# Gathers of a graph network issued in quarters that wait for the turn, and with a pause in the middle of each group

## The chip, the cores and the metric

The kernel runs on one core of a Trainium2 chip. The metric is the device time in microseconds of one execution. The core has five engines with queues of their own: TensorE (PE; its weight loads are PEld), VectorE (DVE), ScalarE (ACT), GpSimd (POOL) and SyncE (SP), which here only issues transfers. They meet through semaphores: an instruction, or a transfer that has landed, adds to one, and another engine waits until it has reached a value.

## The reference

Four graph layers over 6250 nodes with 256 features and 106250 edges in order of their destination. Cut to what matters:

```python
edge_index = jnp.stack([src, dst])
h = jnp.maximum(_layernorm(x), 0.0)
# two convolution layers, for each: x = x + relu(segment_sum(h[row] * norm[:, None], col) + b),
# with h = layer_norm(x) @ W.T; after the second one x @ Wp.T + bp
x = x + _L0_gnn_ref(h, edge_index, edge_weight, ...)
h = jnp.maximum(_layernorm(x), 0.0)
# attention layer with 4 heads, then a transformer layer with one head:
#   alpha = segment_softmax(leaky_relu(a_src[src] + a_dst[dst]), dst)
#   x1    = prelu(segment_sum(h[src] * alpha, dst) + bias)
#   alpha2 = segment_softmax(q[dst] . k[src] * scale, dst)
#   out   = prelu(segment_sum(v[src] * alpha2, dst) + x1 @ Wskip + bskip)
x = x + _L1_gnn_ref(h, edge_index, ...)
```

## The kernel before

The edges are cut into 52 groups of 2048 (`NGW` = 52): 128 partitions times 16 columns (`UW` = 16). The kernel runs four layers one after the other, each as a loop of 52 turns, one turn for each group. In this data a group's destinations lie within one window of 128 nodes (the work on a window's nodes is recorded 53 times in a layer: 52 groups and the end); loops for more windows stand in the code.

For each group GpSimd issues 16 gathers, one for each column: each fetches 128 rows of a node table in HBM (256 to 264 numbers of 4 bytes), by the source indices of the column, into `G[:, b, u]`. `G` has four buffers (`NBW` = 4), so the gathers of group g go where group g - 4 was, and they are issued while the turn of group g - 3 runs. A quarter is four columns (`QW` = 4). GpSimd does nothing but issue these gathers.

- **Convolution layers 1 and 2** (`first_layer`, `second_layer`). GpSimd waits, ahead of a group's first gather, until ACT has added to `s_done` for group g - 4 (L800, L1114), then issues all 16 (L227, L849). In a turn VectorE makes 16 one-hot matrices `oh` (L577, L947), TensorE multiplies each with a column of `G` and sums into `ps` (L727, L1069; it signals each quarter through `s_ohu`), ScalarE copies the sum to `stage` (the eviction, L799, L1112; it waits for all four signals), and TensorE, ScalarE and VectorE work out the window's nodes from it. The landing of each quarter has its own semaphore, `s_g[b][q]`.
- **Attention layer** (`gat_layer`, called layer 3 here). VectorE adds the logits `L` once the whole group has landed (`s_g[b]`, one semaphore for a group) and the scores `psA` are there, runs maxima along the edges (`F`, `W`), and signals `s_s1`; TensorE turns the ends (L1586, L1587, signal `s_rt`), VectorE carries the maxima over the partitions (`run`, `Out`, signal `s_s2`), TensorE turns them back (L1594, L1595, signal `s_bt`), VectorE works out `M` and `z`, ACT the exponentials. Then VectorE writes `Gp` from `M` (L1490, signal `s_lastM`) and weighs `G` into `Gp` in four quarters (L1390, signal `s_gp` each). One turn later TensorE adds up `oh` times `Gp` (L1561), a quarter at a time, each with the signal `s_aq`. VectorE makes the next group's `oh` quarter q only when `s_aq` tells that the old one was read (L1279). TensorE then makes the next group's scores (L1519) and the node's products (L1527 to L1539). GpSimd waits once in a group, for `s_gp` of group g - 4, and issues all 16 gathers (L1192).
- **Transformer layer** (`transformer_layer`, layer 4). Not touched. Its gathers already wait at each quarter, for `s_aq` of that quarter, and at the first also for `s_ok`.

SyncE loads and stores the nodes' rows of each window. An engine's queue is in program order; nothing but the semaphores orders the engines against each other.

Of the kernel before, what the change touches and what calls it, by code (L numbers as in the profile page):

```python
# [43 lines left out]
NBW = 4  # L44
QW = 4
# [72 lines left out]
def first_layer(nc, m, a):  # L118
# [13 lines left out]
    with ExitStack() as c:  # L132
# [48 lines left out]
        s_g = [[sem(f"gath{b}{q}") for q in range(UW // QW)] for b in range(NBW)]  # L181
# [17 lines left out]
        @block.gpsimd  # L199
        def _(pool):  # L200
            nc.gpsimd.memset(m.ones[:], 1.0)
            nc.gpsimd.memset(m.eps[:], LN_EPS)
            nc.gpsimd.memset(m.ident[:], 0.0).then_inc(s_set, 1)
            pool.wait_ge(s_set, 1)
            nc.gpsimd.affine_select(out=m.ident[:], in_=m.ident[:], compare_op=ALU.not_equal, fill=1.0,
                                    base=0, pattern=[[-1, P]], channel_multiplier=1)
            nc.gpsimd.iota(m.iota[:], [[1, P]], base=0, channel_multiplier=0, allow_small_or_imprecise_dtypes=True)
            nc.gpsimd.iota(m.iotap[:], [[1, 1]], base=0, channel_multiplier=1, allow_small_or_imprecise_dtypes=True)
            nc.gpsimd.memset(stage[:], 0.0)
            nc.gpsimd.memset(al[:], 0.0)  # L210
            nc.gpsimd.memset(h[:, :, D:AW], 0.0)
            nc.gpsimd.memset(zrow[:], 0.0).then_inc(s_set, 1)
            nc.gpsimd.memset(acc, 0.0).then_inc(s_accz, 1)
            pool.wait_ge(s_si, 16)
            pool.wait_ge(s_z1, 16)
            pool.wait_ge(s_ast, 16)
            for j in range(NLB):
                pool.wait_ge(s_t1[j], 16)
            for g in range(NGW):
                b = g % NBW  # L220
                width = D if g < NBW else AW
                if g >= NBW:
                    pool.wait_ge(s_done, g - NBW + 1)
                if g == NBW:
                    pool.wait_ge(s_col, 16)
                for u in range(UW):
                    pool.indirect_dma_start(G[:, b, u, 0:width], None, m.t1,  # L227
                                            IOA(ap=m.srcI[:, g * UW + u:g * UW + u + 1], axis=0)).then_inc(s_g[b][u // QW], 16)

# [575 lines left out]
def second_layer(nc, m, a_in):  # L805
# [5 lines left out]
    with ExitStack() as c:  # L811
# [14 lines left out]
        s_g = [[sem(f"gath{b}{q}") for q in range(UW // QW)] for b in range(NBW)]  # L826
# [14 lines left out]
        @block.gpsimd  # L841
        def _(pool):
            nc.gpsimd.memset(stage[:], 0.0).then_inc(s_zero, 1)
            for g in range(NGW):
                b = g % NBW
                if g >= NBW:
                    pool.wait_ge(s_done, g - NBW + 1)
                for u in range(UW):
                    pool.indirect_dma_start(G[:, b, u, :], None, table, IOA(ap=m.srcI[:, g * UW + u:g * UW + u + 1],  # L849
                                                                            axis=0)).then_inc(s_g[b][u // QW], 16)  # L850

# [268 lines left out]
def gat_layer(nc, m):  # L1120

    tag = "g3_"
    LD, ST, NQ = 16, 48, UW // QW
    GL = UW * 16
    SW = HC + 1
    with ExitStack() as c:
# [21 lines left out]
        s_g = [sem(f"gath{b}") for b in range(NBW)]  # L1148
# [32 lines left out]
        @block.gpsimd  # L1181
        def _(pool):
            nc.gpsimd.memset(run[:], -BIG)
            nc.gpsimd.memset(Lb[:], -BIG)
            nc.gpsimd.memset(t4[:], 1.0)
            nc.gpsimd.memset(stage[:], 0.0).then_inc(s_zero, 1)
            for g in range(NGW):
                b = g % NBW
                if g >= NBW:
                    pool.wait_ge(s_gp, (g - NBW + 1) * NQ)  # L1190
                for u in range(UW):
                    pool.indirect_dma_start(G[:, b, u, :], None, m.t3, IOA(ap=m.srcI[:, g * UW + u:g * UW + u + 1],  # L1192
                                                                           axis=0)).then_inc(s_g[b], 16)

# [1179 lines left out]
```

## Time and profile before

| | |
|---|---|
| time, median of 3 runs | 6131.06 us (6126.41 to 6134.06) |
| profiled execution: its time | 6161.81 us |
| its span, first to last instruction | 6160.0 us |
| mean granted TensorE clock | 0.761 of full speed |
| PE busy | 3909.5 us (63%) |
| PEld busy | 2847.9 us (46%) |
| DVE busy | 2717.3 us (44%) |
| ACT busy | 718.7 us (12%) |
| POOL busy | 3225.9 us (52%) |

No engine is busy all the time. "Busy" leaves out waits, branches and the issuing of SyncE's transfers. A wait in the profile is named after the last update of a semaphore that the profile can find; semaphore numbers are used again by the next layer, so a wait can be put down to a tile of another layer. "issue" and "remote" are waits for which it finds no instruction. The ends of matmuls are modelled.

### The profile page before, as it was taken

What the parts mean: (1) busy time and instruction counts of PE and PEld (TensorE: products, weight loads), DVE (VectorE), ACT (ScalarE), POOL (GpSimd) and SP (SyncE); (2) the same over time, 40 slices, a digit from 0 to 9 for tenths busy, and PEclk for the clock granted to TensorE, in tenths of its full rate; (3) what the DMA queues carried; (4) which work ended last, traced back from release to release, by engine and by line L of the source; (5) the groups of instructions that cost most, each with busy time, mean ns of one, the idle gap of its engine ahead of it and who ended that gap; (6) DMA issues with size and microseconds to landing.
All of it is one profiled execution on the core that took longest, in us unless ns stands there. A gap on an engine that the chain in (4) does not pass through costs nothing. (4 is left out here: it accounts for less than half of the span.)

```text
span 6160.0 us, 73788 instructions
## 1 busy us (share of the span) xinstructions
PE 3909.5 (63%) x14574; PEld 2847.9 (46%) x14575; DVE 2717.3 (44%) x9904; ACT 718.7 (12%) x2361; POOL 3225.9 (52%) x3351
## 2 busy tenths in 40 slices
PE   3555555563665566654676766666674777777777
PEld 2343434342444344443555555555552555555555
DVE  5443434343233323332444444444453555555555
ACT  3000000000000000000111111101010222121222
POOL 5466666645555555655444444444423555555553
PEclk8677777776777777776777777777776888888889
DMA  7344444433333333333333333333322344444442
GB/s 182 80 107 106 107 106 107 106 87 90 108 108 107 105 106 107 108 99 90 89 91 100 91 98 91 98 94 96 96 75 85 109 122 115 119 119 114 121 114 84
DMA packets 334355, 636.43 MB, mean 103 GB/s; under 512 B 86166, under 2 KB 213124, under 8 KB 333828
## 3 DMA queue, kind: packets, MB, share of 16 engines
q0 software_dynamic: 159744, 441.43, 27.7%
q1 hardware_dynamic: 170437, 185.56, 9.7%
q8 instruction: 177, 2.90, 0.2%
q10 hardware_dynamic: 3648, 3.67, 0.2%
q14 instruction: 349, 2.86, 0.2%
HBM read 565.59 MB, written 64.79 MB: 102 GB/s over the span
## 5 line engine op out<-in xcount | busy, mean ns | idle before, releaser
L1192 POOL DMA_INDIRECT g_G<-t,srcI x832 | 810.2, 974 | 925.1 <-DVE g_Gp L1390 686.1
L1785 POOL DMA_INDIRECT g_G<-t,srcI x832 | 791.5, 951 | 626.3 <-PE g_ps L2152 365.5
L227 POOL DMA_INDIRECT g_G<-t,srcI x832 | 818.5, 984 | 518.8 <-issue 238.5
L849 POOL DMA_INDIRECT g_G<-t,srcI x832 | 796.4, 957 | 541.2 <-ACTq L1114 302.3
L2142 PE MATMUL g_psA<-g_win,g_ohT 128*128 128x257 f32 x1664 | 613.9, 456 | 369.6 <-issue 187.0
L727 PE MATMUL g_ps<-g_G,g_oh 128*128 128x257 f32 x1664 | 550.3, 496 | 141.7 <-DVE g_oh L577 139.3
L1519 PE MATMUL g_psA<-g_win,g_ohT 128*128 128x4 f32 x1664 | 345.1, 328 | 439.0 <-issue 429.1
L1887 DVE CUSTOM_DVE_ANT_0 g_junk<-g_G,g_psA 128x257 f32<-128x257 f32 x832 | 348.0, 418 | 569.2 <-DMA g_G<-t,srcI 245.8
L1519 PEld LDWEIGHTS g_psA<-g_win,g_ohT 128*128 128x128 f32 x1664 | 360.1, 317 | 459.5 <-issue 459.2
L2152 PE MATMUL g_ps<-g_G,g_oh 128*128 128x257 f32 x1664 | 560.1, 423 | 2.3 <-issue 2.3
L2142 PEld LDWEIGHTS g_psA<-g_win,g_ohT 128*128 128x128 f32 x1664 | 319.1, 216 | 503.0 <-issue 232.1
L727 PEld LDWEIGHTS g_ps<-g_G,g_oh 128*128 128x128 f32 x1664 | 412.3, 256 | 287.5 <-DVE g_oh L577 182.6
L1069 PE MATMUL g_ps<-g_G,g_oh 128*128 128x256 f32 x1664 | 517.7, 460 | 0.0
L1069 PEld LDWEIGHTS g_ps<-g_G,g_oh 128*128 128x128 f32 x1664 | 379.2, 237 | 97.2 <-issue 34.8
L1561 PE MATMUL g_ps<-g_Gp,g_oh 128*128 128x264 f32 x1664 | 408.1, 393 | 15.9 <-issue 15.8
L2152 PEld LDWEIGHTS g_ps<-g_G,g_oh 128*128 128x128 f32 x1664 | 353.5, 215 | 86.7 <-issue 26.2
L1279 DVE TENSOR_TENSOR g_oh<-iota,g_relx 128x512 f32<-128x512 f32 x208 | 135.5, 689 | 562.5 <-DMA g_G<-t,srcI 519.7
L1561 PEld LDWEIGHTS g_ps<-g_Gp,g_oh 128*128 128x128 f32 x1664 | 310.8, 192 | 95.8 <-issue 43.8
L947 DVE TENSOR_SCALAR g_oh<-iota,g_relx,g_wx 128x128 f32<-128x128 f32 x832 | 229.0, 350 | 141.5 <-issue 75.5
L584 DVE SCALAR_TENSOR_TENSOR g_a<-g_own,g_stage 128x256 f32<-128x256 f32 x53 | 25.7, 485 | 566.6 <-ACT g_stage L799 565.1
L964 DVE TENSOR_TENSOR g_o<-g_psP,g_xb 128x256 f32<-128x256 f32 x53 | 22.5, 425 | 535.7 <-DMA g_srow<-srow 444.7
L577 DVE TENSOR_SCALAR g_oh<-iota,g_relx,g_wx 128x128 f32<-128x128 f32 x832 | 239.9, 363 | 32.5 <-issue 22.6
(373 smaller groups left out, 5050.1 us busy)
## 6 DMA issues: line engine op xcount, KB each, us to landing
g_G<-t,srcI POOLq DMA_INDIRECT x3328
g_relb<-relrow SPq DMA_DIRECT2D x104, 512.0 KB
t<-g_t SPq DMA_DIRECT2D x53, 132.0 KB
g_rec<-t SPq DMA_DIRECT2D x53, 132.0 KB
g_own<-t SPq DMA_DIRECT2D x53, 129.5 KB
x<-g_o SPq DMA_DIRECT2D x53, 128.5 KB
g_rec<-x SPq DMA_DIRECT2D x53, 128.5 KB
t<-g_t4r SPq DMA_DIRECT2D x53, 128.5 KB
```

The lines of the kernel that those rows point to most:

```text
L227: pool.indirect_dma_start(G[:, b, u, 0:width], None, m.t1, IOA(ap=m.srcI[:, g * UW + u:g * UW + u + 1], axis=0)).then_inc(s_g[b][u // QW], 16)
L577: nc.vector.tensor_scalar(oh[:, u, :], m.iota[:], relx[:, u:u + 1], wx[:, u:u + 1], ALU.is_equal, ALU.mult).then_inc(s_oh, 1)
L727: last = nc.tensor.matmul(ps[:, 0:CW], oh[:, u, :], G[:, b, u, 0:CW], start=(u == 0), stop=(u == UW - 1))
L849: pool.indirect_dma_start(G[:, b, u, :], None, table, IOA(ap=m.srcI[:, g * UW + u:g * UW + u + 1], axis=0)).then_inc(s_g[b][u // QW], 16)
L1069: last = nc.tensor.matmul(ps[:, 0:D], oh[:, u, :], G[:, b, u, :], start=(u == 0), stop=(u == UW - 1))
L1192: pool.indirect_dma_start(G[:, b, u, :], None, m.t3, IOA(ap=m.srcI[:, g * UW + u:g * UW + u + 1], axis=0)).then_inc(s_g[b], 16)
L1519: last = nc.tensor.matmul(psA[:, u * H:u * H + H], ohT[:, u, :], win[:, b % 2, :], start=True, stop=True)
L1561: last = nc.tensor.matmul(ps[:, 0:AGW], oh[:, b1, u, :], Gp[:, b1, u, :], start=(u == 0), stop=(u == UW - 1))
L1785: pool.indirect_dma_start(G[:, b, u, :], None, m.t4, IOA(ap=m.srcI[:, g * UW + u:g * UW + u + 1], axis=0)).then_inc(s_g[b][u // QW], 16)
L1887: nc.vector.tensor_tensor_reduce(out=junk[:, u % 2, :], in0=G[:, b, u, :], in1=psA[:, u % 2, 0:RW], scale=1.0, scalar=0.0, op0=ALU.mult, o ...
L2142: nc.tensor.matmul(psA[:, u % 2, 0:RW], ohT[:, u, :], win[:, r, :], start=True, stop=True).then_inc(s_pa, 1)
L2152: last = nc.tensor.matmul(ps[:, r, 0:RW], oh[:, b2, u, :], G[:, b2, u, :], start=(u == 0), stop=(u == UW - 1))
```

## The change

- In both convolution layers GpSimd waits once more in each group from the fifth on: ahead of the ninth gather, until the second quarter of this same group (gathers 5 to 8) has landed.
- In the attention layer the single wait ahead of a group is split into four, one ahead of each quarter: the first as before (`s_gp`: group g - 4 has been weighed), the second for `s_aq` of the second quarter of group g - 4 (TensorE has added up half of it), the third for `s_s2` and the fourth for `s_lastM` of group g - 3, whose turn is running.

```diff
--- before.py
+++ after.py
@@ -224,6 +224,8 @@
                 if g == NBW:
                     pool.wait_ge(s_col, 16)
                 for u in range(UW):
+                    if g >= NBW and u == 2 * QW:
+                        pool.wait_ge(s_g[b][1], (g // NBW + 1) * 16 * QW)
                     pool.indirect_dma_start(G[:, b, u, 0:width], None, m.t1,
                                             IOA(ap=m.srcI[:, g * UW + u:g * UW + u + 1], axis=0)).then_inc(s_g[b][u // QW], 16)
 
@@ -846,6 +848,8 @@
                 if g >= NBW:
                     pool.wait_ge(s_done, g - NBW + 1)
                 for u in range(UW):
+                    if g >= NBW and u == 2 * QW:
+                        pool.wait_ge(s_g[b][1], (g // NBW + 1) * 16 * QW)
                     pool.indirect_dma_start(G[:, b, u, :], None, table, IOA(ap=m.srcI[:, g * UW + u:g * UW + u + 1],
                                                                             axis=0)).then_inc(s_g[b][u // QW], 16)
 
@@ -1186,9 +1190,16 @@
             nc.gpsimd.memset(stage[:], 0.0).then_inc(s_zero, 1)
             for g in range(NGW):
                 b = g % NBW
-                if g >= NBW:
-                    pool.wait_ge(s_gp, (g - NBW + 1) * NQ)
                 for u in range(UW):
+                    if g >= NBW:
+                        if u == 0:
+                            pool.wait_ge(s_gp, (g - NBW + 1) * NQ)
+                        elif u == QW:
+                            pool.wait_ge(s_aq, (g - NBW) * NQ + 2)
+                        elif u == 2 * QW:
+                            pool.wait_ge(s_s2, g - NBW + 2)
+                        elif u == 3 * QW:
+                            pool.wait_ge(s_lastM, g - NBW + 2)
                     pool.indirect_dma_start(G[:, b, u, :], None, m.t3, IOA(ap=m.srcI[:, g * UW + u:g * UW + u + 1],
                                                                            axis=0)).then_inc(s_g[b], 16)
```

## Rows read from the trace of the kernel before

**Rows 1.** One line's instructions: attention gathers, duration in ns, first and last start.

```profile
L1192 POOL DMA_INDIRECT g_G<-t,srcI x832: 940/946/3132, 2825.7 to 4559.9; - x167
```

**Rows 2.** Waits, whole run: us in total, times, longest us.

```profile
ACT g_stage L799 <- remote: 807.7, 48, 17.6
...
DVE g_oh L1279 <- DMA g_G<-t,srcI: 519.7, 55, 14.2
...
DVE g_o L964 <- DMA g_srow<-srow: 444.7, 38, 50.4
```

**Rows 3.** ScalarE's timeline, evictions: start us, us, what [idle before].

```profile
211.49 0.39 ACT L799 ACTIVATE g_stage<-g_ps 128x257 f32<-128x257 f32 x1 [11.34 <-PE g_ps L727]
...
1349.11 0.39 ACT L799 ACTIVATE g_stage<-g_ps 128x257 f32<-128x257 f32 x1 [16.86 <-remote]
...
1402.38 0.39 ACT L799 ACTIVATE g_stage<-g_ps 128x257 f32<-128x257 f32 x1 [11.34 <-PE g_ps L727]
...
1512.74 0.38 ACT L1112 ACTIVATE g_stage<-g_ps 128x256 f32<-128x256 f32 x1 [3.30 <-PE g_ps L1069]
...
2759.97 0.38 ACT L1112 ACTIVATE g_stage<-g_ps 128x256 f32<-128x256 f32 x1 [3.25 <-PE g_ps L1069]
...
2806.10 0.38 ACT L1112 ACTIVATE g_stage<-g_ps 128x256 f32<-128x256 f32 x1 [2.07 <-PE g_ps L1069]
...
2947.47 0.39 ACT L1654 ACTIVATE g_stage<-g_ps 128x264 f32<-128x264 f32 x1 [0.16 <-DVE g_v L1339]
...
4568.17 0.39 ACT L1654 ACTIVATE g_stage<-g_ps 128x264 f32<-128x264 f32 x1 [0.20 <-DVE g_v L1339]
...
4632.10 0.39 ACT L1654 ACTIVATE g_stage<-g_ps 128x264 f32<-128x264 f32 x1 [0.20 <-issue]
...
5320.39 0.39 ACT L2240 ACTIVATE g_stage<-g_ps 128x257 f32<-128x257 f32 x1 [2.19 <-PE g_ps L2152]
...
5428.56 0.39 ACT L2240 ACTIVATE g_stage<-g_ps 128x257 f32<-128x257 f32 x1 [6.48 <-PE g_ps L2152]
...
6087.60 0.39 ACT L2240 ACTIVATE g_stage<-g_ps 128x257 f32<-128x257 f32 x1 [1.57 <-PE g_ps L2152]
...
6130.22 0.39 ACT L2240 ACTIVATE g_stage<-g_ps 128x257 f32<-128x257 f32 x1 [0.33 <-PE g_ps L2152]
```

**Rows 4.** Timeline of one turn of layer 1: GpSimd, ScalarE, TensorE.

```profile
852.00 0.94 POOL L227 DMA_INDIRECT g_G<-t,srcI  x1 [3.83 <-ACTq L800]
...
870.93 0.95 POOL L227 DMA_INDIRECT g_G<-t,srcI  x1 [0.30 <-issue]
...
868.93 0.70 PE L727 MATMUL g_ps<-g_G,g_oh 128*128 128x257 f32 x2
...
875.10 0.39 ACT L799 ACTIVATE g_stage<-g_ps 128x257 f32<-128x257 f32 x1 [16.71 <-remote]
```

**Rows 5.** Timeline of one turn of the attention layer: GpSimd, TensorE, VectorE.

```profile
3573.68 0.94 POOL L1192 DMA_INDIRECT g_G<-t,srcI  x1 [15.01 <-DVE g_Gp L1390]
...
3584.45 0.71 PE L1561 MATMUL g_ps<-g_Gp,g_oh 128*128 128x264 f32 x2
...
3587.39 0.17 PE L1519 MATMUL g_psA<-g_win,g_ohT 128*128 128x4 f32 x1 [1.99 <-issue]
...
3596.70 1.89 DVE L1279 TENSOR_TENSOR g_oh<-iota,g_relx 128x512 f32<-128x512 f32 x3 [12.81 <-DMA g_G<-t,srcI]
```

**Rows 6.** Timeline in layer 4: first and last of eight gathers, VectorE.

```profile
5299.91 0.95 POOL L1785 DMA_INDIRECT g_G<-t,srcI  x1 [2.12 <-PE g_ps L2152]
...
5308.72 0.95 POOL L1785 DMA_INDIRECT g_G<-t,srcI  x1 [0.30 <-issue]
...
5311.47 0.42 DVE L1887 CUSTOM_DVE_ANT_0 g_junk<-g_G,g_psA 128x257 f32<-128x257 f32 x1 [2.91 <-DMA g_G<-t,srcI]
```

**Rows 7.** Timeline, attention layer's first group: its sixteenth gather and who awaits it.

```profile
2846.65 0.94 POOL L1192 DMA_INDIRECT g_G<-t,srcI  x1 [0.30 <-issue]
...
2849.57 0.27 DVE L1406 TENSOR_TENSOR g_L<-g_G,g_psA 128x64 f32<-128x64 f32 x1 [16.56 <-DMA g_G<-t,srcI]
```

## The prediction

> **What bounds the kernel now.** I read the page first, then the waits, then the timelines of single turns. The page shows no busy engine (PE 63%, POOL 52%), so the time lies in waits. The waits [rows 2] show where: ScalarE waits 807.7 us in 48 pieces, 16.8 us each, to evict layer 1's sum; VectorE waits 519.7 us in layer 3 to refill its one-hots; and 444.7 us in layer 2 for TensorE's second product. Two of these are named after a DMA, but the instructions wait for TensorE's signals (`s_aq`, `s_prod2`); I go by the code.
>
> The timelines say what those signals wait for. In layer 1 a group's first gather starts at 852.00, the last matmul of the running sum ends at 868.93 + 0.70 = 869.63, and nothing but TensorE's signal is missing; yet the eviction starts at 875.10, 5.5 us later and 23.10 us after the first gather [rows 4]. In layer 3 the matmuls of the sum end at 3585.16, but VectorE's refill of quarters 2 to 4 starts at 3596.70, 11.5 us later and 23.02 us after the first gather [rows 5]; TensorE's small score matmuls are meanwhile issued 2 us apart (1.99 us idle ahead of the one at 3587.39). In layer 4, whose gathers come in quarters already, eight in a row start at 5299.91, and the wait behind them ends at 5311.47, after 11.56 us [rows 6]. 23.10/16, 23.02/16 and 11.56/8 are all 1.44 us. So I read: while GpSimd gathers without a break, TensorE's signals are held back, and they are let go 1.44 us times the number of gathers after the first. GpSimd itself needs (870.93 - 852.00)/15 = 1.262 us a gather [rows 4], 20.19 us a group; the attention layer's gathers are the same in length, 946 ns of work each in the median of 832 [rows 1], and the rest is a 0.30 us gap ahead of each.
>
> How much this costs can be read off the end of each layer, where the last turns run with no gathers beside them. From eviction to eviction [rows 3]:
> - layer 1: (1349.11 - 211.49)/48 = 23.70 us with gathers, (1402.38 - 1349.11)/3 = 17.76 without
> - layer 2: (2759.97 - 1512.74)/48 = 25.98 and (2806.10 - 2759.97)/3 = 15.38
> - layer 3: (4568.17 - 2947.47)/47 = 34.48 and (4632.10 - 4568.17)/3 = 21.31
> - layer 4: (5428.56 - 5320.39)/4 = 27.04 and (6130.22 - 6087.60)/2 = 21.31
>
> Layers 1 to 3 bind themselves to it: the eviction (or the weighing, in layer 3) sets off the next burst of 16, and the burst holds back the next eviction.
>
> **Conv layers: the pause.** Nothing is removed; 48 waits are added in each layer. Behind the wait in GpSimd's queue stand only gathers, for data that is used three turns later. The wait's price is GpSimd's idle time. The one landing that an engine visibly waits for is that of layer 3's first group: its sixteenth gather starts at 2846.65, and VectorE goes on at 2849.57, 2.92 us later [rows 7]. The eighth gather of a group starts 7 x 1.262 = 8.83 us after the first, so it is known to have landed at 11.75 us; the ninth would have started at 10.09. The pause is 1.66 us, and a group takes GpSimd 20.19 + 1.66 = 21.85 us at least. That is the floor of a turn. The first eight's hold ends at 8 x 1.44 = 11.56 us, just within the pause, so the second half starts with the signals free. The Trainium skill (DMA: Bandwidth & Descriptors, "Anatomy of one DMA — SWDGE (gpsimd) path") fits such a transfer with 2.0 us plus bytes/436 GB/s, an estimate of 2.3 us for 128 KB; by it the pause would be 1.0 us and would end inside the first half's hold. The row has the longer time and decides.
>
> - Layer 1: between 23.70 (no gain) and 21.85. The sum's last matmul ends 17.63 us after the first gather [rows 4], 5.9 us into the second half. If that signal is held to the second half's end, 11.75 + 11.56 = 23.3 us, the turn is as long as before; if it gets through, evictions run ahead and the turn falls to the floor for good, as three buffers are in hand. I can't tell which, so I take the middle: 22.8, a gain of 0.9 x 48 = 43 us.
> - Layer 2: between 25.98 and 21.85. It loses twice in a turn, at the second product [rows 2] and at the eviction. The first is clearly in the first half and is freed by 11.56; the second is as in layer 1. Without holds its turn is only 15.38, so more margin is there than in layer 1. I take 23.2, two thirds of the way: 2.8 x 48 = 133 us.
>
> **Attention layer: four gates.** One wait in 48 groups becomes four. Again only gathers stand behind them. They need to be issued by the turn's end: 20.19 us of issuing fit into 34.48 and still into 22. The landing is needed two turns after the last gate, so lateness costs nothing. The gates fall like this in a turn: quarter 1 when the weighing ends, quarter 2 when half of the sum is added (some 8 to 10 us on, so quarter 1 stands alone and its hold is over at 4 x 1.44 = 5.8), quarter 3 at `s_s2`, which has then passed, so right behind quarter 2; quarter 4 at `s_lastM`, then the next quarter 1. So two groups of eight take the place of one of sixteen, each with a hold that ends at 11.56 instead of 23.02 us. The refill and `s_bt`, due some 5 us into the first eight, come up to 6.7 us late instead of 11.5.
>
> The nearest rows for the result are layer 4's: quarters, in fours and eights, and there a turn takes 27.04 - 21.31 = 5.7 us more than without gathers [rows 3]. With it layer 3's turn is 21.31 + 5.7 = 27.0, a gain of 7.4 x 47 = 350 us. Bounds: no gain at 34.48, and 22, where GpSimd's 20.19 and TensorE's 21.31 meet, 12.5 x 47 = 590 us.
>
> **Sum.** 43 + 133 + 350 = 526 us. The profiled execution would go from 6161.81 to 5636. It lies 30.75 us above the median 6131.06; with the same saving the median becomes 5605.
>
> **Rivals.**
> 1. *Layer 3's quarters join up* (5840). If `s_bt` comes through early, `s_lastM` comes before the hold of quarters 2 and 3 has ended, quarter 4 follows without a gap, then the next quarter 1: again 16 in a row and a hold of 23 us, now over the node's products. I reckon some 32 us a turn: 2.5 x 47 = 118, with the conv layers' 176, 294. For it: layer 3's plain turn is nearly as short as GpSimd's 20.19. Against it: held signals delay `s_lastM` themselves, which separates the bursts again.
> 2. *The pause doesn't take in the conv layers* (5780): the late signal stays held to 23.3 us in each turn, or the second half starts before the first's hold is over, as only 11.75 against 11.56 us speaks for it. Layer 3's 350 us remain.
> 3. *The waits have nothing to do with bursts* (6131, no change). Gatherless turns are shorter in all four layers, by 6 to 13 us, which speaks against it. The Trainium skill (SBUF — State Buffer, "Who interferes with whom") says that DMA never contends with a compute engine and that PE never waits on anyone; by that rule moving gathers about would change nothing. Rows 4 and 5 disagree with the rule as far as TensorE's signals go: 5.5 and 11.5 us between matmul and signal.
> 4. *Slower: the hold ends a fixed time after the last gather, wherever it is* (6290). In layer 1 the eviction starts 875.10 - 871.88 = 3.2 us after the last gather's end [rows 4]. If that is the law, the pause moves each eviction and so each turn by its 1.66 us: 96 x 1.66 = 159 us, layer 3 unchanged. It decides from any pause at all, since the next burst waits for the eviction. Against it: behind eight gathers it is 5311.47 - 5309.67 = 1.8 us [rows 6], not 3.2; the delay grows with the burst, as 1.44 - 1.262 = 0.18 us a gather does.
>
> **How the numbers follow.** Forecast 0.60, rival 1 0.16, rival 2 0.14, rival 3 0.04, rival 4 0.06. Under 0.2% (12 us) a measurement of this kernel can't tell a change from none. The forecast's own range is 5420 to 5720: layers 1 and 2 both at the floor give 89 + 198 instead of 176, and layer 3 anywhere from 25 to 29 a turn. The whole range is 5400 to 5850, which takes in rivals 1 and 2 and leaves 3 and 4 outside. Faster 0.90, same 0.04, slower 0.06.
>
> **What would show it.** In the profile after: GpSimd's ninth gather in the conv layers has an idle time of 1.5 to 2 us ahead of it. Layer 1's evictions come 21.9 to 23.7 us apart, layer 2's 21.9 to 24.5, layer 3's about 27, layer 4's 27.0 as before. The wait of L1279 falls from 519.7 us to below 250, that of L964 to below 300. In layer 3 GpSimd's gathers stand in fours and eights, not in sixteens. The prediction fails if layer 3's turn stays above 31, if signals are held as long behind eight gathers as behind sixteen, or if GpSimd becomes the bound of layer 3 with landings waited for at L1406.

## The result, and the profile after

The change makes the kernel slower: 6246.22 us (median of 4, 6226.23 to 6287.01) against 6130.16 (6126.41 to 6134.06), ratio 1.0205, 95% interval 1.0168 to 1.0242. The forecast was 5605 us. The profiled execution takes 6287.01 us, its span is 6285.1 us, and the mean granted clock is 0.734 (0.761 before).

ScalarE's timeline after, first and last eviction of layers 1 and 2, and in layer 3 the first one and the one 47 turns later (start us, us, what [idle before]):

```profile
212.04 0.39 ACT L801 ACTIVATE g_stage<-g_ps 128x257 f32<-128x257 f32 x1 [11.34 <-PE g_ps L729]
...
1397.52 0.39 ACT L801 ACTIVATE g_stage<-g_ps 128x257 f32<-128x257 f32 x1 [11.21 <-PE g_ps L729]
...
1508.76 0.38 ACT L1116 ACTIVATE g_stage<-g_ps 128x256 f32<-128x256 f32 x1 [4.27 <-PE g_ps L1073]
...
2838.84 0.38 ACT L1116 ACTIVATE g_stage<-g_ps 128x256 f32<-128x256 f32 x1 [2.06 <-PE g_ps L1073]
...
2964.70 0.39 ACT L1665 ACTIVATE g_stage<-g_ps 128x264 f32<-128x264 f32 x1 [0.16 <-issue]
...
4676.32 0.39 ACT L1665 ACTIVATE g_stage<-g_ps 128x264 f32<-128x264 f32 x1 [0.20 <-issue]
```

Against [rows 3]: layer 1 takes 1185.5 us instead of 1190.9, layer 2 1330.1 instead of 1293.4, and the 47 turns of layer 3 1711.6 instead of 1620.7 (36.42 us a turn instead of 34.48). So most of the loss is in the attention layer, some in layer 2. The profiled execution of before is some 30 us longer than its median, so small differences from it mean little: in the runs below that leave layer 1 alone it takes 1184.8 to 1185.9 us on the chips with the same time, as after the change. The waits after (us in total, times, longest):

```profile
POOL g_G L1203 <- PE g_ps L1572: 761.8, 48, 17.7
ACT g_lt L1653 <- remote: 653.4, 43, 15.7
...
PE g_psO L1546 <- ACT g_lt L1653: 471.7, 43, 11.4
...
DVE g_o L968 <- DMA g_srow<-srow: 339.1, 31, 48.8
...
DVE g_o L968 <- PE g_psP L1034: 232.5, 22, 16.6
...
DVE g_oh L1290 <- DMA g_G<-t,srcI: 20.1, 5, 4.9
```

The refill's wait, 519.7 us before [rows 2], is nearly gone (L1290, 20.1; under all the names that the profile gives this wait, 103.4 instead of 556.7). In its place TensorE itself waits 11 us in 43 turns, at L1546, for ScalarE to take the node's turned rows, and ScalarE waits for TensorE's signal of them. The turn did not get shorter; the held signal is another one.

GpSimd (POOL), ScalarE and TensorE in layer 3, where that happens:

```profile
3508.52 0.94 POOL L1203 DMA_INDIRECT g_G<-t,srcI  x1 [17.61 <-PE g_ps L1572]
...
3527.48 0.95 POOL L1203 DMA_INDIRECT g_G<-t,srcI  x1 [0.30 <-issue]
3546.08 0.95 POOL L1203 DMA_INDIRECT g_G<-t,srcI  x1 [17.66 <-PE g_ps L1572]
...
3531.62 0.38 ACT L1653 ACTIVATE g_lt<-g_psN 128x256 f32<-128x256 f32 x1 [15.48 <-remote]
...
3532.15 2.05 PE L1546 MATMUL g_psO<-gq,g_lt 128*128 128x257 f32 x4 [11.31 <-ACT g_lt L1653]
```

Quarter 2 begins at 3508.52, and from there to 3527.48 sixteen gathers stand 0.30 us apart: quarters 2, 3, 4 and the next 1. TensorE's signal of the turned rows, which were done before 3520.84 (11.31 us ahead of 3532.15), reaches ScalarE at 3531.62, 23.10 us after the burst's first gather, as behind the sixteen of [rows 4, 5]. From there it is 14.46 us until half of the next sum is added and quarter 2 may start again (3546.08). 23.10 + 14.46 is the 37.56 us of most turns. Before, the way from the release to the next burst was 34.48 - 23.02 = 11.46 us.

Layer 1, two turns: first GpSimd, then ScalarE and TensorE.

```profile
856.29 0.95 POOL L229 DMA_INDIRECT g_G<-t,srcI  x1 [0.30 <-issue]
859.30 0.95 POOL L229 DMA_INDIRECT g_G<-t,srcI  x1 [2.06 <-DMA g_G<-t,srcI]
...
868.09 0.95 POOL L229 DMA_INDIRECT g_G<-t,srcI  x1 [0.30 <-issue]
872.22 0.95 POOL L229 DMA_INDIRECT g_G<-t,srcI  x1 [3.18 <-ACTq L802]
...
884.25 0.95 POOL L229 DMA_INDIRECT g_G<-t,srcI  x1 [2.16 <-DMA g_G<-t,srcI]
...
903.58 0.95 POOL L229 DMA_INDIRECT g_G<-t,srcI  x1 [0.30 <-issue]
906.67 0.95 POOL L229 DMA_INDIRECT g_G<-t,srcI  x1 [2.15 <-DMA g_G<-t,srcI]
...
871.72 0.39 ACT L801 ACTIVATE g_stage<-g_ps 128x257 f32<-128x257 f32 x1 [23.59 <-remote]
...
891.08 0.39 ACT L801 ACTIVATE g_stage<-g_ps 128x257 f32<-128x257 f32 x1 [12.48 <-issue]
...
918.96 0.39 ACT L801 ACTIVATE g_stage<-g_ps 128x257 f32<-128x257 f32 x1 [21.69 <-remote]
...
905.54 8.06 PE L729 MATMUL g_ps<-g_G,g_oh 128*128 128x257 f32 x22 [6.54 <-DVE g_oh L579]
```

The group from 872.22 has its pause (2.16 us idle at 884.25), and its eviction comes after only 19.36 us, at 891.08. But then GpSimd is still busy with the group's second half, and when that is through the next group is already free: from 884.25 to 903.58 sixteen gathers run without a break. The next turn meets two holds, this one (TensorE waits 6.54 us for one-hots, whose refill waits for its own signals) and that of the eight behind it (from 906.67, its sum is let go 12.29 us later), and takes 27.88 us. Short and long turns alternate through the whole layer, 23.6 us in the mean. Layer 2 alternates in the same way.

**Which signals are held.** Not every signal of a burst. Two signals of the turn in [rows 4], whose burst of sixteen starts at 852.00; each time the engine that gives it and ScalarE, which waits for it:

```profile
852.91 0.42 PE L699 MATMUL g_psT<-ident,g_a 128*128 128x128 f32 x1
...
853.46 0.38 ACT L784 ACTIVATE g_w6r<-g_psT 128x256 f32<-128x256 f32 x1 [1.58 <-PE g_psT L699]
...
857.78 0.18 DVE L597 BATCH_NORM_AGGREGATE g_mv<-g_st 128x2 f32<-128x6 f32 x1
...
858.09 0.29 ACT L787 ACTIVATE g_sd<-g_mv,eps 128x1 f32<-128x1 f32 x1 [4.25 <-DVE g_mv L597]
```

TensorE's signal, 1.3 us into the burst, takes 0.13 us, and so does VectorE's, 6.0 us into it. The count over before's layers 1 to 3 (250 to 4560 us) says the same: of ScalarE's and VectorE's waits that ended with a TensorE signal, the 202 whose matmul ended in the first 7 us of a burst of sixteen were released within 1.3 us, 187 of them within 0.5; the 92 whose matmul ended 11 to 19 us into it came 4.2 to 12.2 us late, and 87 of these were released 22.7 to 23.4 us after the burst's first gather. Between 7 and 11 us some pass and some don't. ScalarE's and VectorE's own signals, 7 to 20 us into such bursts, took under 0.5 us in 182 of 188 waits. So it is only TensorE's signals, and only those given late in a burst. In layer 3 after the change the turned rows are given 10.7 us into the burst in the median of 48 turns, too late to pass.

### The profile page after: what moved, and what is told of

It is laid out like the page before. It is cut to its first block and busy times, and to the rows that moved or that the text cites. A ratio compares the mean times of both kernels' runs of the same rounds, so it can differ in the third digit from the quotient of the medians.

```text
span 6285.1 us, 73788 instructions
## 1 busy us (share of the span) xinstructions
PE 4072.8 (65%) x14574; PEld 2840.1 (45%) x14575; DVE 2726.9 (43%) x9904; ACT 722.5 (11%) x2361; POOL 3227.9 (51%) x3351
## 5 line engine op out<-in xcount | busy, mean ns | idle before, releaser
L729 PE MATMUL g_ps<-g_G,g_oh 128*128 128x257 f32 x1664 | 606.8, 531 | 278.8 <-DVE g_oh L579 249.7
L2163 PE MATMUL g_ps<-g_G,g_oh 128*128 128x257 f32 x1664 | 564.8, 427 | 2.5 <-issue 2.5
L2153 PEld LDWEIGHTS g_psA<-g_win,g_ohT 128*128 128x128 f32 x1664 | 321.6, 218 | 502.5 <-DVE g_L L1898 236.4
L1572 PE MATMUL g_ps<-g_Gp,g_oh 128*128 128x264 f32 x1664 | 460.9, 431 | 0.7 <-issue 0.7
L1572 PEld LDWEIGHTS g_ps<-g_Gp,g_oh 128*128 128x128 f32 x1664 | 356.1, 219 | 122.6 <-issue 52.8
L1546 PE MATMUL g_psO<-gq,g_lt 128*128 128x257 f32 x212 | 105.0, 648 | 471.7 <-ACT g_lt L1653 471.7
L1546 PEld LDWEIGHTS g_psO<-gq,g_lt 128*128 128x128 f32 x212 | 62.5, 320 | 556.2 <-issue 546.6
L579 DVE TENSOR_SCALAR g_oh<-iota,g_relx,g_wx 128x128 f32<-128x128 f32 x832 | 234.7, 354 | 135.8 <-issue 122.9
L968 DVE TENSOR_TENSOR g_o<-g_psP,g_xb 128x256 f32<-128x256 f32 x53 | 22.5, 425 | 571.6 <-DMA g_srow<-srow 339.1
L2255 ACT ACTIVATE g_oh<-g_oh,g_p 128x128 f32<-128x128 f32 x832 | 248.7, 387 | 6.4
L1873 DVE TENSOR_SCALAR g_oh<-iota,g_relx 128x128 f32<-128x128 f32 x832 | 245.2, 296 | 0.4 <-issue 0.4
L1401 DVE TENSOR_TENSOR g_Gp<-g_G,g_psP 128x1024 f32<-128x1024 f32 x208 | 239.4, 1213 | 1.8 <-ACT g_pf L1692 1.8
```

What stands on the lines that cost most here:

```text
L729: last = nc.tensor.matmul(ps[:, 0:CW], oh[:, u, :], G[:, b, u, 0:CW], start=(u == 0), stop=(u == UW - 1))
L1572: last = nc.tensor.matmul(ps[:, 0:AGW], oh[:, b1, u, :], Gp[:, b1, u, :], start=(u == 0), stop=(u == UW - 1))
L1873: return nc.vector.tensor_scalar(oh[:, b % 4, u, :], m.iota[:], relx[:, b % 2, u:u + 1], None, ALU.is_equal)
L2153: nc.tensor.matmul(psA[:, u % 2, 0:RW], ohT[:, u, :], win[:, r, :], start=True, stop=True).then_inc(s_pa, 1)
L2163: last = nc.tensor.matmul(ps[:, r, 0:RW], oh[:, b2, u, :], G[:, b2, u, :], start=(u == 0), stop=(u == UW - 1))
L2255: last = nc.scalar.activation(src[:, u, :], src[:, u, :], ACT.Copy, scale=p[:, r, u:u + 1])
```

## The experiments

All times are medians; each ratio is against runs of the kernel before on the same chip. The runs of the experiments fell on six chips. On four of them the kernel before takes about 6130 us (6131.21, 6130.68, 6125.80) or 6081.61, and TensorE's signals are held; on two it takes 4473.35 and 4474.26, and no signal is held in the traces from there. Each chip was met only once, so the runs can't tell what belongs to the chip from what belongs to the hour or to other work beside it; "chip" below means both. The first table is of the chips with holds. Layers 1 and 2 are from the first to the last eviction of the profiled run, layer 3 is the mean of its first 47 turns, all in us.

| run | time | ratio (95% interval) | layer 1 | layer 2 | layer 3, a turn |
|---|---|---|---|---|---|
| before | 6131.06 | | 1190.9 | 1293.4 | 34.48 |
| changed | 6246.22 | 1.0205 (1.0168 to 1.0242) | 1185.5 | 1330.1 | 36.42 |
| e1_conv_only | 6174.99 | 1.0084 (1.0051 to 1.0117) | 1184.7 | 1338.7 | 34.14 |
| e2_att_only | 6202.15 | 1.0104 (1.0069 to 1.0139) | 1184.8 | 1285.7 | 36.30 |
| e3_q4_after_lt | 5722.86 | 0.9332 (0.9308 to 0.9356) | 1184.9 | 1291.8 | 26.07 |
| e4_long_pause | 6077.36 | 0.9920 (0.9897 to 0.9944) | 1188.7 | 1225.5 | 34.14 |
| e9_pause_twice_again | 5606.69 | 0.9155 (0.9130 to 0.9180) | 1179.4 | 1171.7 | 25.78 |
| e10_sixteen_at_lt_again | 6078.24 | 0.9919 (0.9897 to 0.9940) | 1185.2 | 1284.5 | 33.33 |
| e13_changed_again | 6249.17 | 1.0202 (1.0161 to 1.0243) | 1187.5 | 1311.3 | 35.67 |
| e14_two_gates_third | 5739.95 | 0.9363 (0.9331 to 0.9395) | 1185.3 | 1289.0 | 26.18 |
| e15_narrow_third | 6131.85 | one run | 1185.9 | 1286.8 | 34.25 |
| e16_changed_third | 6012.23 | 0.9837 (0.9802 to 0.9873) | 1178.3 | 1309.0 | 32.54 |
| e17_q4_after_lt_again | 5660.16 | 0.9305 (0.9282 to 0.9328) | 1177.4 | 1283.1 | 25.53 |

The rows of a layer that a run leaves alone are the better yardstick, since before's profile is of a long execution: layer 1 takes 1184.8 to 1185.9 there, layer 2 1284.5 to 1291.8, layer 3 34.14 to 34.25 a turn (e16 and e17, on the chip with 6081.61, apart). So the change costs nothing in layer 1, 20 to 54 us in layer 2 (e13, changed, e1) and 1.4 to 2.3 us a turn in layer 3.

**One part at a time.** e1 takes the four gates out of the changed kernel, e2 the two pauses.

> The changed kernel with the attention layer's gathers as before: only the pause in the two convolution layers is left. Theory A (the two parts do not interact; the loss lies mostly in the attention layer): layer 1's evictions end some 5 us earlier than before, layer 2's some 37 us later, so about 6160 us, ratio 1.005, and both layers' turns alternate between short and long ones. Theory B (the slower attention layer is an effect of how layer 2 leaves the table or the clock): this kernel takes the whole loss, 6246 us.

> The changed kernel without the pause in the convolution layers: only the attention layer's four gates are left. Theory A (no interaction): layers 1 and 2 as before, layer 3's turn 36.4 us instead of 34.5, about 6230 us, ratio 1.016, with most bursts in layer 3 of sixteen gathers (quarters 2, 3, 4 and the next 1) and the node's turned rows (the signal of the two transposes) held until 23 us after quarter 2 began. Theory B (interaction): within 0.3% of before.

1.0084 and 1.0104 make up the 1.0205 within their intervals: the runs show no interaction of the parts, and both lose. The gates cost less than I had put down for them (71 us of 100), the pauses more (44 of 30).

**The fourth gate moved.** e3 has one new count in ScalarE's queue, behind the eviction that waits for the node's turned rows, and quarter 4 waits for it instead of for `s_lastM`:

```diff
-                            pool.wait_ge(s_lastM, g - NBW + 2)
+                            pool.wait_ge(s_ltk, g - NBW + 1)
...
                 if agg:
                     node_evict(n1)
+                    act.sem_inc(s_ltk, 1)
```

> Convolution layers as before; in the attention layer the fourth quarter waits for ScalarE to have taken the node's turned rows (a count added behind the eviction that waits for TensorE's signal) instead of for the ends of M. Theory A (TensorE's signals are held while a burst lasts, and the loss is that quarter 4 joins quarters 2 and 3 just ahead of the node's signal): bursts of eight, 2+3 and 4+1; the node's signal comes 12 to 13 us after quarter 2 instead of 23; layer 3's turn 27 to 29 us instead of 34.5, about 5850 us (5800 to 5900). Theory B (what is held is only moved on: the second burst of eight now holds the factor's and the row's signals that come 8 to 13 us after it): turn 31 to 34, 5980 to 6120 us. Theory C (the order of the gates does not matter, the gates themselves cost): 36.4 as with the change, 6230 us.

Layer 3 falls from 34.48 to 26.07 us a turn and the kernel by 6.7%. Of the three theories only A fits, though it was too careful: its range was 27 to 29 us a turn and 5800 to 5900 us. The prediction's 27.0 for bursts of eight was near. GpSimd's bursts and ScalarE's eviction of the turned rows in e3:

```profile
3548.48 0.94 POOL L1200 DMA_INDIRECT g_G<-t,srcI  x1 [4.21 <-ACTq L1701]
...
3560.41 0.94 POOL L1200 DMA_INDIRECT g_G<-t,srcI  x1 [1.97 <-PE g_ps L1569]
...
3573.00 0.94 POOL L1200 DMA_INDIRECT g_G<-t,srcI  x1 [2.80 <-ACTq L1701]
...
3572.70 0.38 ACT L1650 ACTIVATE g_lt<-g_psN 128x256 f32<-128x256 f32 x1 [3.39 <-PE g_psN L1535]
```

Eight gathers, a gap of 2 to 4 us, eight gathers; the turned rows come 12.29 us after quarter 2's first gather instead of 23.10. e17 repeats it on another chip:

> Convolution layers as before, quarter 4 of the attention layer behind ScalarE's eviction of the node's turned rows. If before takes about 4473 us on this chip: Theory A (its gates are passed before GpSimd reaches them): no change, ratio within 0.3% of 1. Theory B (the gate comes too late for GpSimd, which sets the turn there): 1 to 3% slower. If before takes about 6130 us here: 5723 us, ratio 0.933, again.

Its ratio is 0.9305, its layer 3 takes 25.53 us a turn. e14 leaves out the third quarter's gate:

> The kernel with quarter 4 of the attention layer behind ScalarE's eviction and without the third quarter's gate. If before takes about 6130 us here: Theory A (only where the two bursts of eight begin counts): 5723 us, 5705 to 5740. Theory B (each gate helps): 5760 us or more. If before takes about 4473 us here: no change.

0.9363 against 0.9332, with intervals that overlap: the third gate does nothing that could be measured.

**Place without splitting.** e10 has one wait for all sixteen gathers, for `s_gp` and the new count together.

> The same kernel as in the earlier run in which the attention layer's sixteen gathers stay together and begin behind ScalarE's eviction of the node's turned rows. If before takes about 6130 us here: Theory A (a hold lasts 23 us from the first gather wherever it begins): 30 us a turn, 5920 us (5850 to 5980). Theory B (splitting is all): 6131. Theory C (the place is all): 5723. If before takes about 4473 us here: no change.

GpSimd and VectorE in its layer 3:

```profile
3519.04 0.94 POOL L1194 DMA_INDIRECT g_G<-t,srcI  x1 [13.22 <-ACTq L1695]
...
3552.40 0.95 POOL L1194 DMA_INDIRECT g_G<-t,srcI  x1 [12.18 <-DVE g_Gp L1392]
...
3542.95 1.90 DVE L1281 TENSOR_TENSOR g_oh<-iota,g_relx 128x512 f32<-128x512 f32 x3 [9.80 <-DMA g_G<-t,srcI]
```

Of theory A the way it counts is right, and one of its terms is not: the refill, which waits for TensorE's signal, starts 23.9 us after the burst's first gather (whose second comes 1.2 us later than usual), about the 23 us that A has; but from there to the next burst it is 9.45 us, not 7; 33.4 in all. The earlier start buys 1.15 us a turn (ratio 0.9919). Splitting is worth the rest.

**A longer pause.** e4 has the attention layer as before, and in the pause of the convolution layers also a GpSimd write of 1.5 us:

```diff
                     if g >= NBW and u == 2 * QW:
                         pool.wait_ge(s_g[b][1], (g // NBW + 1) * 16 * QW)
+                        nc.gpsimd.memset(pz[:], 0.0).then_inc(s_pz, 1)
+                        pool.wait_ge(s_pz, g - NBW + 1)
```

> Attention layer as before; in the convolution layers the pause ahead of the ninth gather is made longer by a GpSimd write of about 1.5 us behind the landing, 3.7 us in all instead of 2.1. Theory A (a hold ends 2.5 to 3.2 us after the last gather of a burst, so the pause of 2.1 us was too short to end it): the signals are let go in every pause, turns no longer alternate, layer 1 at 24.0 to 24.5 us (20 to 40 us slower in all), layer 2 at 24.2 to 25.5 instead of 26.0 (20 to 90 us faster), in all -70 to +20 us against before. Theory B (the hold does not end in a pause at all but with the group's last landing): each turn is longer by the pause, 48 x 3.7 = 178 us in each layer, up to 6480 us. Theory C (the hold counts gathers in flight, pauses change nothing): turns alternate as with the change and are 0.7 to 1.6 us longer on average.

Faster by 0.8%, all of it in layer 2 (1225.5 against 1293.4, 24.0 us a turn from end to end); layer 1 stays, where theory A had it 20 to 40 us slower. GpSimd, ScalarE and TensorE in its layer 2, the eight gathers of a group's second half:

```profile
2014.77 0.95 POOL L859 DMA_INDIRECT g_G<-t,srcI  x1 [0.27 <-POOL g_pz L857]
...
2026.28 0.38 ACT L1122 ACTIVATE g_stage<-g_ps 128x256 f32<-128x256 f32 x1 [5.39 <-DMA g_G<-t,srcI]
...
2022.22 0.70 PE L1079 MATMUL g_ps<-g_G,g_oh 128*128 128x256 f32 x2
```

The sum ends at 2022.92, its signal comes at 2026.28, 11.51 us after the first of the eight. A longer pause beats the shorter one, which speaks against B, and against C for layer 2. Theory A's mark, that turns no longer alternate, did not come either: in layer 2 they take 17.2, 31.8 and 25.3 us by turns. This kernel too has no pause between groups, and the next run adds one.

**A second pause, between the groups.** e9 is e3 with a wait at each group's first gather as well:

```diff
+                if g >= NBW:
+                    pool.wait_ge(s_g[(g - 1) % NBW][3], ((g - 1) // NBW + 1) * 16 * QW)
                 for u in range(UW):
+                    if g >= NBW and u == 2 * QW:
+                        pool.wait_ge(s_g[b][1], (g // NBW + 1) * 16 * QW)
```

> The same kernel as in the earlier run with two pauses in a group, which fell on a chip where the kernel before takes 4473 us and TensorE's signals are not held. If before takes about 6130 us here: Theory A (bursts of eight with 2.1 us behind them are let go in time): 5640 us (5600 to 5690), layer 1's turn 23.7 to 24.3, layer 2's 23.7 to 24.8, no alternation. Theory B (turns alternate as with the change): 5740 to 5780 us. If before takes about 4473 us here: again 4882 us, since 96 groups pay two pauses of 2.1 us each.

5606.69 us, 8.5% faster than before and the fastest run on these chips. GpSimd and ScalarE in its layer 2:

```profile
2010.84 0.94 POOL L857 DMA_INDIRECT g_G<-t,srcI  x1 [2.59 <-DMA g_G<-t,srcI]
...
2022.98 0.94 POOL L857 DMA_INDIRECT g_G<-t,srcI  x1 [2.19 <-DMA g_G<-t,srcI]
...
2035.19 0.94 POOL L857 DMA_INDIRECT g_G<-t,srcI  x1 [2.53 <-DMA g_G<-t,srcI]
...
2014.93 0.38 ACT L1120 ACTIVATE g_stage<-g_ps 128x256 f32<-128x256 f32 x1 [5.07 <-issue]
...
2039.00 0.38 ACT L1120 ACTIVATE g_stage<-g_ps 128x256 f32<-128x256 f32 x1 [6.62 <-PE g_ps L1077]
```

Each burst has eight gathers, evictions come 24.07 us apart, and from the twentieth turn of layer 2 on nothing alternates; in the turns ahead of it the first groups, which have no pauses, are used up (16 to 23 us each). A group takes GpSimd 24.35 us (2010.84 to 2035.19), and it waits for an eviction in only one group of layer 2: it is the bound now. Layer 2 gains 122 us, layer 1 11 (113 to 120 and some 6 against the runs that leave them alone).

**Bytes or gathers.** e15 is the kernel before, with layer 2's gathers from the fifth group on cut to 64 of 256 columns:

> The kernel before with layer 2's gathers from the fifth group on cut to 64 of the 256 columns (the output is not the reference's). If before takes about 6130 us here: Theory A (a hold goes with the number of gathers): layer 2's evictions 25 to 26 us apart, signals 22.5 to 23 us after the first gather. Theory B (it is a backlog of bytes): the turn is 15.4 to 24 us and signals come earlier. If before takes about 4473 us here: 19.9 to 20.2 us a turn.

The same stretch of layer 2 in e15 and in before (us, busy times, granted clock, DMA share, GB/s), and one burst of e15:

```profile
1507.00:2669.00 1162.00, 718.20 (x2342) 505.13 (x2341) 362.54 (x1264) 100.16 (x271) 684.54 (x720) 0.74 0.20 46
```

```profile
1513.00:2670.00 1157.00, 690.57 (x2327) 488.99 (x2325) 355.52 (x1244) 99.66 (x268) 683.92 (x715) 0.75 0.37 107
```

```profile
2024.00 0.94 POOL L849 DMA_INDIRECT g_G<-t,srcI  x1 [6.36 <-ACTq L1114]
...
2046.90 0.38 ACT L1085 ACTIVATE g_lt<-g_psT 128x256 f32<-128x256 f32 x1 [7.60 <-remote]
```

46 GB/s instead of 107, and the signal still comes 22.9 us after the burst's first gather; the layer takes 1286.8 us, as where it is left alone. A hold goes with the number of gathers in a row (or of the rows that they fetch, 128 each, which was not varied), not with their bytes.

**Chips without holds.** e5, e6, e7 and e8 were the kernels of e9, e14, e10 and e15, and e11 and e12 repeated e6 and e8; all six met a chip on which before takes 4473 or 4474 us.

> The kernel with quarter 4 of the attention layer behind ScalarE's eviction (5723 us), and in both convolution layers two waits for landed gathers in a group: ahead of the ninth gather as in the change, and a second one ahead of the first, for the last gathers of the group before. Theory A (the loss of layer 2 is that the change's pause stands only in the middle: when a turn is short the next group follows without a break, sixteen gathers in a row are held 23 us, and the 2.1 us pause behind them ends before the 3.05 us that their signals need): every burst has eight gathers and its signals come 11.5 us after its first, in each pause; no alternation; layer 1's turn 23.7 to 24.0 (two times 11.84), layer 2's 23.7 to 24.8 instead of 25.9, so 5640 us (5600 to 5690). Theory B (the hold does not end in pauses of 2.1 us): turns alternate as with the change, 5740 to 5780 us.

> As the kernel with quarter 4 behind ScalarE's eviction, with the third quarter's gate (the maxima carried over the partitions) left out, so that quarter 3 follows quarter 2. Theory A (what counts is only where the two bursts of eight begin): the third gate never waits, no change against 5723 us, 5705 to 5740. Theory B (each gate spreads the gathers and so shortens a hold): slower, 5760 us or more.

> Convolution layers as before; in the attention layer all sixteen gathers of a group stay together, but begin when ScalarE has taken the node's turned rows, some 4.5 us earlier in the turn than before. Theory A (a hold lasts 23 us from the first gather, wherever it begins, and the turn is that plus the way from the release to the next start): 23.0 plus 7 us, 30 us a turn instead of 34.5, 5920 us (5850 to 5980). Theory B (splitting is all, the place does not matter): no change, 6131 us. Theory C (the place is all, splitting adds nothing): 26 us a turn, 5723 us.

> The kernel before, but in layer 2 every gather from the fifth group on fetches only the first 64 of the 256 columns (a quarter of the bytes, the same number of rows; the other columns of G stay as the first four groups left them, so the output is not the reference's). Theory A (a hold lasts as long as descriptors of gathers are made and worked off, whatever their bytes): TensorE's signals still come 22.5 to 23 us after the first gather, layer 2's turn 25 to 26 us. Theory B (the hold is the transfers' backlog, 1.44 us of data for each gather against 1.26 of issuing): signals come 21 to 21.5 us after the first gather at most, or are not held at all, and the turn is between 15.4 and 24 us.

> The kernel with quarter 4 of the attention layer behind ScalarE's eviction and without the third quarter's gate, once more. If before takes about 6130 us here: Theory A (only where the two bursts of eight begin counts): 5723 us as with the gate, 5705 to 5740. Theory B (each gate helps by spreading gathers): 5760 us or more. If before takes about 4473 us here: no change, as in the first run.

> The kernel before with layer 2's gathers from the fifth group on cut to 64 of the 256 columns, once more (the output is not the reference's; the other columns of G stay as the first four groups left them). If before takes about 6130 us here: Theory A (a hold goes with the making and working off of descriptors, whatever their bytes): layer 2's evictions still 25 to 26 us apart and TensorE's signals 22.5 to 23 us after the first gather. Theory B (the hold is a backlog of bytes): the turn is 15.4 to 24 us and signals come earlier. If before takes about 4473 us here: layer 2's turn 19.9 to 20.2 us, set by GpSimd, as in the first run.

e5: 4882.52 us, ratio 1.0904 (1.0886 to 1.0922). e6: 4473.69, 1.0003 (0.9994 to 1.0013); e7: 4473.57, 0.9996 (0.9986 to 1.0006); e11: 4474.30, 0.9996 (0.9986 to 1.0006); e8 and e12, one run each: 4471.85 and 4468.60. The theories of e5 to e8 were not tested there, since there was nothing held. One turn of layer 1 in e6, to be laid beside [rows 4]:

```profile
909.20 0.70 PE L727 MATMUL g_ps<-g_G,g_oh 128*128 128x257 f32 x2
...
910.04 0.39 ACT L799 ACTIVATE g_stage<-g_ps 128x257 f32<-128x257 f32 x1 [13.19 <-PE g_ps L727]
...
908.97 0.94 POOL L227 DMA_INDIRECT g_G<-t,srcI  x1 [0.30 <-issue]
910.22 0.94 POOL L227 DMA_INDIRECT g_G<-t,srcI  x1 [0.30 <-issue]
```

The sum's last matmul ends at 909.90 and the eviction starts 0.14 us later, not 5.5, with GpSimd gathering without a break on both sides. TensorE's clock doesn't explain it: the granted clock is 0.76 over this layer (200 to 1100 us), 0.72 over the same layer before (300 to 1300 us), and the pair of matmuls takes 0.70 us in both. GpSimd sets every turn there (layer 3: 20.73 us in e6; sixteen gathers are 20.2; it idles only the usual 0.30 us ahead of each), so whatever makes it pause is paid in full: e5's 192 pauses (two in each of 96 groups) cost 409 us, 2.13 us each, and gates that GpSimd finds open cost nothing.

**The changed kernel elsewhere.** e13 and e16 are the changed kernel again.

> The changed kernel itself. If before takes about 4473 us on this chip (no signal held): Theory A (where nothing is held GpSimd's gathers set the turn, so a pause adds its own length): 96 pauses of 2.1 us add 202 us and the gates of the attention layer nothing, 4675 us (4660 to 4700). Theory B (the gates wait for the turn, which is nearly as short as GpSimd's 20.2 us, so they add too): 4700 to 4900 us. If before takes about 6130 us here: 6246 us again, layer 1 -5, layer 2 +37, layer 3 +100 us.

> The changed kernel. If before takes about 4473 us on this chip (no signal held): Theory A (GpSimd's gathers set the turn, so a pause adds its own length): 96 pauses of 2.1 us add 202 us and the gates nothing, 4675 us (4660 to 4700). Theory B (the gates add too, since the turn is nearly as short as GpSimd's 20.2 us): 4700 to 4900 us. If before takes about 6130 us here: 6246 us a third time.

e13 gives 1.0202, as at first. e16 met the chip with 6081.61, and there the same kernel is faster than before, against what was expected: its ten runs go from 5925.12 to 6078.07, a spread of 2.5%. Their median is 1.1% below before's; the ratio 0.9837 leaves the four longest out. The profiled run took 6026.11. The two profiles differ in how often quarter 4's gate was waited for at all, first in the changed kernel's own profile, then in e16's:

```profile
POOL g_G L1203 <- DVE g_Gp L1501: 18.5, 8, 3.2
```

```profile
POOL g_G L1203 <- DVE g_Gp L1501: 46.8, 25, 3.5
```

In 8 against 25 of 48 turns (GpSimd idles for over 1 us ahead of quarter 4 in 11 against 22). In the first profile each of the 36 turns with an open gate takes 37.4 to 37.6 us, counted from quarter 2 to quarter 2; the five whose gate holds GpSimd for 2.9 us or more take 27.5 to 27.7; and the six with some 1.2 us take 37.3 to 37.5, so a break that short doesn't part a burst. In e16 the turns go from 24 to 38. The changed kernel stands on an edge. What tips it there is not shown; a hold a little shorter may (layer 1's turn is 23.4 us in e17 on that chip, and 23.6 on the others, with the same gathers). On the two chips without holds the changed kernel wasn't run; its 96 pauses at 2.13 us would make it some 204 us slower there, an estimate.

## Why the prediction was wrong

- **The reading of before was right as to when held signals are let go**, on the chips that it was made on: 23.10 us after the first of sixteen gathers (layer 3 after) (22.9 in e15), and 11.51 us after the first of eight (e4). It was too wide in that it has all of TensorE's signals held while GpSimd gathers; those given in the first 7 us pass. Rival 3 falls: moving gathers moves the time by up to 8.5%. The rule behind it, that DMA contends with no compute engine and that PE waits on nobody (the Trainium skill, SBUF — State Buffer, "Who interferes with whom"), disagrees with the traces of four chips and agrees with those of two.
- **The step that failed** is in "Attention layer: four gates": "quarter 4 at `s_lastM`, then the next quarter 1. So two groups of eight take the place of one of sixteen". I placed the gates by the turn before the change. But quarter 2's gate opens late, when half the sum is added, its and quarter 3's gathers take 10 us, and by then `s_lastM` is mostly there: it was waited for in 8 of 48 turns. So sixteen stay together, and the node's turned rows fall into their held part. Rival 1 had this mechanism, with the hold "over the node's products", and only 0.16. Its price, 32 us a turn, was too low: the turn is the hold plus the way from the release to the next start, 23.10 + 14.46 = 37.56, and quarter 2's gate is a worse starting point than the weighing's end (11.46). I had counted only how late the signals are, not what starts the next burst.
- **The size behind that step was right.** With two bursts of eight layer 3's turn is 26.07, 26.18, 25.53 and 25.78 us (e3, e14, e17, e9), against 27.0 forecast. That e9, with working gates and two pauses, lands at 5606.69 us, on the forecast 5605, is partly luck: layer 3's 47 turns gain 409 us instead of 350, and the convolution layers 133 instead of 176.
- **Convolution layers: the floor.** The pause's length was near: 1.66 us forecast on top of the usual 0.30, 1.86 measured (2.16 idle), and an eighth gather's landing 3.01 us after its start (856.29 to 859.30 in layer 1's timeline). The estimate of 2.3 us by the Trainium skill (DMA: Bandwidth & Descriptors, "Anatomy of one DMA — SWDGE (gpsimd) path") is too short when counted from the gather's start, as the prediction counts it; from the end of GpSimd's 0.95 us of work on it, the landing takes 2.06. What failed is "evictions run ahead and the turn falls to the floor for good, as three buffers are in hand". The one thing that had parted the groups was the wait for the eviction. Once evictions run ahead it is gone, and the second half joins the next group's first. Whether the pause behind such sixteen gathers is also too short is argued and not shown: by [rows 4] a held signal needs 875.10 - 871.88 = 3.2 us from the last gather's end and the pause has 2.1, but in the long turn shown above TensorE works on through that pause. e9, with a break on both sides, has a floor, at 24 instead of 21.85, since each group pays two pauses.
- **Rival 4** (a fixed time after the last gather, 6290 us) came nearest to the time, for a reason that is not the cause: layer 3, which it left unchanged, holds most of the loss, and e4's longer pause made layer 2 faster, not slower.
- **What was to show it.** The ninth gather's idle time is 2.1 us (1.5 to 2 forecast). L1279's wait fell as forecast and bought nothing; L964's rose (339.1 + 232.5, against 444.7 + 53.9 under the same two names). Layer 3's turn above 31 us was named as a sign of failure, and it was 36.4.
- **Open:** why TensorE's signals pass in the first 7 us of a burst (the eviction at 891.08, too, starts 6.8 us into one), and why in layer 3 after it is one turn in eight that takes 26 us. What TensorE's signals share with the gathers, and why two chips don't show it, no run tells.

## What to carry to other kernels

When a signal is held behind a burst of another engine's work, a turn lasts the hold plus the way from its release to the next burst's start; so look at what starts each burst, and which signal falls into its held part (here what TensorE gives later than 7 us into it), before counting how late anything is. A gate only splits a burst if it is still closed when the queue reaches it: take a signal that comes from behind the hold (here ScalarE's having taken the rows), not one that is early on its own. A pause inside a group does nothing if removing the delay also removes the gap between groups.

And run the same comparison on several chips. Here the change gives +2.0% on some and -1.1 to -1.6% on one, and on chips without holds each pause is pure loss; e3's gates, whose repair is worth 6.7 to 7.0%, are the safe choice, since the like of them cost nothing there, while e9's pauses add 2% to them on chips with holds (5722.86 to 5606.69) and lose 9% on the others.

## What the hardware showed unexpectedly

- The same program takes 6131 us on one chip and 4473 on another. GpSimd's work on a gather (0.94 us, 0.30 gap) and the order are the same; what differs is how long TensorE's signals take: 0.14 us from the matmul's end to the eviction in e6, 5.5 in [rows 4]. Three chips agree within 0.1% (6131.21, 6130.68, 6125.80), two others within 0.03% (4473.35, 4474.26), one takes 6081.61. Whether it is the chip or the hour stays open, as each was met once.
- TensorE's signals are held late in a burst of gathers only: given in the first 7 us they pass within 1.3 us, given 11 to 19 us into sixteen they come 4.2 to 12.2 us late, while ScalarE's and VectorE's pass.
- Quartering the gathers' bytes (107 to 46 GB/s) leaves the holds as long as they were.
- Where holds fall in a kernel's loop can make it bistable: ten runs of the changed kernel on one chip spread over 2.5%, those of before over 0.5%.
